# Where the residual's stores stand in SyncE's queue, at the border into an expert FFN

## The reference

```
xf = layernorm(x).reshape(4096, 256)
Sm = softmax(xf @ Wr + br)                      # 4096 x 8
G_t, idx_t = top_k(Sm.T, 512)                   # each expert chooses its tokens
tokens = xf[idx]
mid = silu(einsum('keh,ehf->kef', tokens, Wu) + bu)     # 256 -> 682
out = einsum('kef,efh->keh', mid, W_down) + b_down      # 682 -> 256
y = zeros_like(xf).at[idx].add(G * out)
x = x + tanh(g_ffn[0]) * y
```

## Time and profile before

| | us |
|---|---|
| runs | 708.39, 709.97, 710.17 |
| median | 709.97 |
| the profiled execution | 709.88 |
| its span in the profile | 708.1 |
| TensorE busy in the span | 640.5 (90%) |
| VectorE busy | 423.5 (60%) |
| ScalarE busy | 303.1 (43%) |
| GpSimd busy | 266.7 (38%) |

### The profile page before, as it was taken

The page is one execution under the profiler, slowest core; times in us unless marked ns, Lnnn a source line. Parts: engine busy times, 40 slices in busy tenths (PEclk is TensorE's granted clock), DMA queues, the critical chain, the costliest instruction groups (busy, mean ns, idle before and its releaser), DMA issues.

```text
span 708.1 us, 14478 instructions
## 1 busy us (share of the span) xinstructions
PE 640.5 (90%) x5191; PEld 464.4 (66%) x5191; DVE 423.5 (60%) x1287; ACT 303.1 (43%) x632; POOL 266.7 (38%) x388
## 2 busy tenths in 40 slices
PE   7899999899999988859999999998899999992990
PEld 5465565677777755547566665656888888881880
DVE  6654766798999758863112222112658988883771
ACT  2323324777888825443212222220465555510660
POOL 4201102454455511042565445333211334355475
PEclk9999999999999999989999999999999999996996
DMA  8639962777774319981463894322723494122752
GB/s 265 213 120 228 204 136 71 124 127 124 135 132 81 107 48 186 245 280 38 82 156 42 242 292 95 73 30 32 236 61 120 150 302 168 61 90 86 215 167 78
DMA packets 101278, 99.95 MB, mean 141 GB/s; under 512 B 22182, under 2 KB 91305, under 8 KB 101204
## 3 DMA queue, kind: packets, MB, share of 16 engines
q1 hardware_dynamic: 91992, 82.57, 45.9%
q0 software_dynamic: 9216, 16.46, 10.3%
HBM read 61.20 MB, written 38.05 MB: 140 GB/s over the span
## 4 chain that ended last, share of the span: by engine, by line
PE 49%; DVE 5%; issue 3%; POOL 2%; DMA 2%; ACT 1%; POOLq 1%; DVEq 0%; ACTq 0%
PE pc L1705 10%; PE pc L1682 8%; PE pc L2265 3%; PE pc L2260 3%; PE pc L2532 3%; PE pc L1065 3%; PE pc L2301 2%; PE pc L2258 2%; PE pc L1658 2%; PE pc L2242 2%; PE pc L1701 1%; PE pc L61 1%; POOL result L2437 1%; PE pc L2323 1%; PE pc L1670 1%
## 5 line engine op out<-in xcount | busy, mean ns | idle before, releaser
L1522 POOL DMA_INDIRECT scratch_resid<-y,k_idx x32 | 54.9, 1716 | 81.8 <-DVE y L1590 81.2
L506 DVE TENSOR_REDUCE neg_max<-pb_two 128x8 f32<-128x1024 f32 x64 | 78.1, 1221 | 12.0 <-PE pb_two L836 9.1
L671 ACT ACTIVATE probs<-pb_two,b_key_cols 128x1024 f32<-128x1024 f32 x64 | 76.9, 1202 | 17.1 <-PE pb_two L860 17.1
L1705 PE MATMUL pc<-w_dn,mid 128*128 128x256 f32 x320 | 73.3, 384 | 0.0
L1633 ACT ACTIVATE mid<-pc,b_up 128x512 f32<-128x512 f32 x35 | 24.1, 687 | 109.7 <-PE pc L1682 109.7
L1705 PEld LDWEIGHTS pc<-w_dn,mid 128*128 128x128 f32 x320 | 59.5, 190 | 12.7 <-issue 5.3
L1682 PE MATMUL pc<-gT,w_up 128*128 128x512 f32 x140 | 61.2, 592 | 0.0
L1590 DVE TENSOR_SCALAR y<-pc,gate 128x256 f32<-128x256 f32 x32 | 15.5, 484 | 64.9 <-PE pc L1705 47.1
L1513 POOL DMA_INDIRECT rows<-scratch_rows,k_idx x32 | 32.0, 999 | 53.6 <-DVE k_idx L1366 38.0
L1682 PEld LDWEIGHTS pc<-gT,w_up 128*128 128x128 f32 x140 | 26.6, 190 | 30.5 <-issue 30.1
L1572 DVE COPY gT<-pc 128x512 f32<-128x512 f32 x7 | 4.8, 692 | 61.0 <-PE pc L1670 61.0
(11 more groups left out here) (381 smaller groups left out, 1417.4 us busy)
## 6 DMA issues: line engine op xcount, KB each, us to landing
qs<-scratch_qparts SPq DMA_DIRECT2D x48, 128.0 KB, 4.2
ks<-scratch_kparts SPq DMA_DIRECT2D x48, 128.0 KB
w_dn<-in_W_down SPq DMA_DIRECT2D x8, 640.0 KB
scratch_slots<-s_zero SPq DMA_DIRECT2D x1, 4160.0 KB, 19.5
cT<-in_ctxT SPq DMA_DIRECT2D x8, 512.0 KB, 6.6
s_x<-in_x SPq DMA_DIRECT2D x8, 512.0 KB, 6.8
scratch_rows<-s_x SPq DMA_DIRECT2D x16, 256.0 KB, 4.1
scratch_resid<-s_x SPq DMA_DIRECT2D x8, 512.0 KB, 7.0
```

Source lines behind the costliest of these rows:

```text
L506: V.tensor_reduce(neg_max[:].rearrange("p (b u j) -> p u b j", b=2, u=2)[:, u], ps_both[0][:].rearrange("p (b j k) -> p b j k", b=2, j=4), ...
L671: A.activation(probs[t % 2 * 2 + u][:], ps_both[1][:].rearrange("p (h q) -> p h q", h=HEADS // 2), ACT.Exp, bias=key_cols[:, 1, t:t + 1], ...
L1522: pool.indirect_dma_start(out=T["resid"], out_offset=bass.IndirectOffsetOnAxis(ap=S["idx"][:, e, c:c + 1], axis=0), in_=y[e % 2][:, c, :], ...
L1705: ins = nc.tensor.matmul(here(c), mid[e % 2][m][:, c * P:(c + 1) * P], w_dn[e % 2][:, m, :], start=False, stop=(m == MT - 2))
```

## The change

SyncE now issues both groups of first weights one after the other. It then waits until each of expert 0's four gathers has landed, and only then issues the residual's eight stores and the two quads of the turned context. The `Stage` object gets a field through which the four semaphores reach the code that writes out SyncE's order. No transfer is added or taken away, and no other engine's instructions change.

```diff
--- before.py
+++ after.py
@@ -1014,8 +1014,8 @@
     def __init__(self, on_sync, on_gpsimd, on_scalar, on_vector, on_tensor, first_weights=None, clear_slots=None, small_loads=None, bulk_loads=None,
                  tables_on_gpsimd=None, tables_on_vector=None, idx_s=None, rows_out=None, cleared_s=None, found_a=None, found_d=None,
                  added=None, all_added=None, sent_s=None, stored_s=None, bias_on_vector=None, last_places=None, last_tiles=None, ones_on_vector=None,
-                 weights_on_scalar=None, all_weights=None):
-        self.weights_on_scalar, self.all_weights = weights_on_scalar, all_weights
+                 weights_on_scalar=None, all_weights=None, first_rows=None):
+        self.weights_on_scalar, self.all_weights, self.first_rows = weights_on_scalar, all_weights, first_rows
         self.on_sync, self.on_gpsimd, self.on_scalar, self.on_vector, self.on_tensor = on_sync, on_gpsimd, on_scalar, on_vector, on_tensor
         self.first_weights, self.clear_slots, self.small_loads, self.bulk_loads = first_weights, clear_slots, small_loads, bulk_loads
         self.tables_on_gpsimd, self.tables_on_vector = tables_on_gpsimd, tables_on_vector
@@ -1724,7 +1724,7 @@
                 turn(e + 1)
             down(e)
 
-    return Stage(on_sync, on_gpsimd, on_scalar, on_vector, on_tensor, first_weights=first_weights, ones_on_vector=ones_on_vector, added=added, all_added=EXPERTS * 16 * ST)
+    return Stage(on_sync, on_gpsimd, on_scalar, on_vector, on_tensor, first_weights=first_weights, ones_on_vector=ones_on_vector, added=added, all_added=EXPERTS * 16 * ST, first_rows=rows_in[0])
 
 
 ROW1 = D + 4
@@ -2641,10 +2641,12 @@
             route.on_sync(sp)
             bidir.small_loads(sp)
             ffn.first_weights(sp, 0)
+            ffn.first_weights(sp, 1)
+            for c in range(CAP // P):
+                sp.wait_ge(ffn.first_rows[c], 16)
             store_residual(sp)
             for q in (0, 1):
                 aside.load_turned(sp, q)
-            ffn.first_weights(sp, 1)
             ffn.on_sync(sp, {4: route.clear_slots, 5: bidir.bulk_loads})
             bidir.on_sync(sp, {4: last.all_weights})
             last.on_sync(sp)
```

## The result

The changed kernel is slower: 714.04 us median (20 runs, 710.16 to 717.42) against 710.15 for the kernel before (20 runs, 706.83 to 712.57). The ratio is 1.0046, with a 95% interval of 1.0030 to 1.0062, so 3.3 us slower by the ratio, which the text goes by (the two medians are 3.9 us apart). 707.1 was forecast, with a range of 705.2 to 709.6.

What follows compares the result with a forecast made beforehand. TensorE carries about half the chain; at the border VectorE idles 2.89 us for expert 0's first gather. 709.88 - 2.9 = 707.0, said as 707.1 because of the median, clock and other costs at about nothing; range 705.2 to 709.6.

Steps and rivals of the forecast that it cites:

- The residual must be landed before the first scatter-add.: Stores moved behind the gathers: last lands at 330.7, GpSimd's first scatter-add is due at 332.9, so it just fits.
- Nothing is added on any other engine: Cost elsewhere: no other engine gets more to do; only four waits and no DMA are new.
- GpSimd's cover of 2 us: Ahead of the first scatter-add: the time left between the last store's landing and GpSimd's need of it.
- The direct gain: Expert 0's first gather lands in 2.8 us, so VectorE starts its first normalising 2.88 us earlier: 2.9 us gained.
- The clock: TensorE around expert 0's first half: clock falls and returns as long behind the restart as before; close to nothing.
- A: Rival: TensorE's clock holds at 2.4 GHz through expert 0's first half; gain 4.2 us, 705.8; chance 0.25.
- B: Rival: TensorE's clock returns late in expert 0's first products; gain 1.7 us, 708.3; chance 0.12.
- Rival C: Expert 0's gathers don't become quicker, the stores being no obstacle; nothing gained, 710.0; chance 0.11.
- Rival D: Expert 1's gathers are held behind the stores, TensorE's turning of expert 1 is 5.1 us late; 712.2; chance 0.07.
- Expert 1's and expert 2's gathers: Issued beside the stores: expert 1's hidden with 2.2 us left, expert 2's delay expert 0's first y 0.8 us; cost 0.
- SyncE's queue: Stores, quads and expert 2's weights behind SyncE's new wait: through by 326.8, nothing late by 24 us.
- the quads' readers: The two turned context quads are first read near 488, so moving them later is free.

Runs made afterwards that it cites:

- e1: The changed kernel with VectorE's wait for the residual's stores (line 1919) moved behind expert 0's outputs; 0.9968 of the kernel before.
- e13: The kernel of e1 run again, beside the changed one; 0.9957 of the kernel before.
- e2: Control: the kernel before with VectorE's wait for the stores moved as in e1, SyncE's order left alone; 1.0008 of the kernel before.
- e5: The kernel of e1 with the nine filling turns issued ahead of TensorE's wait for expert 0's second block; 0.9944 of the kernel before.
- e3: The kernel before with expert 1's weights issued ahead of the residual's stores and no new wait on SyncE; 1.0030 of the kernel before.
- e10: The kernel of e3 run again with more rounds; 0.9997 of the kernel before.
- e11: The changed kernel itself, run again on the chip of three other follow-up runs; 1.0043 of the kernel before.
- second group: Second of three groups of four follow-up runs, each group on one chip beside the kernel before, which took 709.48 us there.

## Why the prediction was wrong

**The step that failed** is the one on the residual: "The residual must be landed before the first scatter-add." The residual's landing was taken to have one reader, GpSimd at line 1534. There is a second one, VectorE at line 1919, and it comes 12 us sooner: 323.7 in the kernel before, where GpSimd's first scatter-add starts at 335.8. With the stores moved, the landing (331.5 measured; 330.7 had been forecast, for indices that came 0.87 us sooner, so it was right to 0.1) was in time for GpSimd, as costed, and 9.7 us too late for VectorE. "Nothing is added on any other engine" is true of instructions. But a wait that had been met when VectorE came to it became one that isn't. No view of the kernel before shows it, since it left no idle time there. It stands in the code, and the timeline of VectorE had its neighbour (the operation of line 1920) without an idle time ahead of it. To look up the semaphore's waiters would have shown it at once. What it did to the time is shown by e1, e13 and e2: with this wait alone out of the way the kernel is faster than before, and the same edit without the late stores does nothing. With it out of the way, GpSimd's cover of 2 us is thin as well: in e5, where the outputs come sooner, the stores are what ends GpSimd's wait ahead of its first scatter-add (7.28 us, to 330.02).

**The direct gain** was right. 2.9 us were forecast. From the indices to the first product the kernel before took 12.4 us. In e13, where the nine turns ran at half clock as they had before, it is 9.7: 2.7 gained. The first gather of the changed kernel took 3.0 us; 2.8 had been taken. What the sum had at nothing without a row is the time ahead of the indices: it let VectorE and ScalarE alone decide when they come, but TensorE's look-up stands on that chain too, and took 0.7 us longer in the changed kernel's execution.

**The clock** did both things that the rivals A and B describe, in different executions. In e1 it stayed up from the first block on, and the first product came 8.1 us behind the indices: 4.3 gained, where A said 4.2. In e13 it came back late. TensorE's timeline:

```profile
313.56 2.18 PE L61 MATMUL pc<-s_ident 128*128 128x128 f32 x9 [0.88 <-DVE xg L1554]
...
317.24 4.82 PE L1658 MATMUL pc<-gT,w_up 128*128 128x256 f32 x16
...
329.78 1.09 PE L1670 MATMUL pc<-s_ident,xg 128*128 128x128 f32 x8
```

Nine turns took 2.18 us, the first 16 products 4.82 instead of 3.6, and expert 1's turning came 22.3 us behind the indices, where it was 23.8 before: 1.5 gained, where B said 1.7. So both prices were right, each in one trace. The changed kernel's own execution lies between: the clock fell near 314.3 and was back near 317.7. The idle ahead of the first transposes, which the forecast put at 1.9 us, was 1.32 there, 0.95 in e1 and 1.70 in e13. As e1 and e13 are one program, which of the three happens is not fixed by the kernel, and the prediction had one execution to judge their chances by.

**Rival C** (gathers not quicker) fell: 3.0 us with the stores out of the way, 4.0 with the quads alone out of the way, 6.5 with neither. The Trainium skill (DMA: Bandwidth & Descriptors, "Queues, rings and completion order") has each DMA engine go round its queues. These three landings do not look like a gather that takes its turn. The other cause that the rival named, a long rest of GpSimd ahead of its first gather, falls too: it had rested 38.68 us in the changed kernel. Gathers issued beside freshly started stores land in 2.7 to 5.4 and 5.2 to 7.1 us, so how long one takes goes with how full the queues are when it comes.

**Rival D** had the right place, TensorE's turning of expert 1, and the right sign, and was given 0.07. Its mechanism was wrong. It held the gathers responsible, which landed in at most 5.4 us, not in the 15.2 that it needed. Its price for a microsecond of lateness was right, but it left out that an idle time of 3.9 us there also takes the clock down, which was worth another 2.7.

**Expert 1's and expert 2's gathers, SyncE's queue, the quads' readers**: no idle time of TensorE at this border goes back to them in the traces, as costed.

## What to carry to other kernels

When a transfer is moved later, list every wait on its semaphore, on every engine, and ask of each when its engine gets there. The wait that cost the time here had left no sign in the trace of the kernel before. The first one reached counts, not the one for which the transfer was made. The two halves of this change also need not go together: moving a fifth of the bytes gave most of the gain, because the gather had only to be landed when the next engine was free.

## What the runs showed of the hardware that was not expected

The place at which TensorE's clock falls and comes back differs between executions of one kernel. In e3 it was down from 304 to 311 and from 317 to 321, and in e10, the same program, from 311.4 to 321.6. Ahead of the indices this cost e3 0.9 us (2.13 us of look-ups for 1.22); behind them it cost e10 0.7 us in the nine turns and 0.7 in the first 16 products (4.82 us for 4.17). Each is a good part of the 3 us under study.

The chips differ more than the kernels do. From the last scatter of the second attention (line 1883) to the end it is 57.4 us in the trace of the kernel before, 58.2 in the changed one's and 57.8 in e2's, but 64.5 in e1's and 65.3 in e11's. In the second group it is 57.5 to 58.9 throughout, in the first and third 63.2 to 67.0, which is about what the medians of the kernel before differ by. Why is open; it was not tried.
